# Cross attention and expert routing on one core: where VectorE picks a batch's experts

## The reference

```
scores = einsum('bhqd,bhkd->bhqk', q, k) * SCALE          # 16 heads of 16
attn = softmax(scores); out = (attn @ v) @ o_w + o_b
x = layernorm(x + out)
logits = x @ gate_w                                       # 8 experts
w, sel = top_k(softmax(logits), 2); w = w / sum(w)
routed = sum over the two chosen experts of w * swiglu_e(x)
```

## Time and profile before

| what | value |
|---|---|
| median of 3 runs | 997.99 us (994.1 to 998.68) |
| profiled execution | 1004.03 us, span of its instructions 1002.2 us |
| TensorE busy | 880.7 us, 88% |
| VectorE busy | 633.7 us, 63% |
| ScalarE busy | 433.4 us, 43% |
| GpSimd busy | 342.8 us, 34% |
| mean granted clock of TensorE | 0.95 |

### The profile page before, as it was taken

How to read it: one execution, slowest core, us unless ns; L and a number is a source line. 1 busy time by engine, 2 the same in 40 slices (tenths; PEclk the granted TensorE clock), 3 DMA queues, 4 the chain that set the end, 5 groups by cost and what they waited for, 6 DMA issues and landing times.

```text
span 1002.2 us, 18341 instructions
## 1 busy us (share of the span) xinstructions
PE 880.7 (88%) x6859; PEld 660.2 (66%) x6859; DVE 633.7 (63%) x1488; ACT 433.4 (43%) x781; POOL 342.8 (34%) x318
## 2 busy tenths in 40 slices
PE   6799788869988888899889998979997999999995
PEld 5576566657766665778656555555785777777774
DVE  5799797666898988852656778773553343333255
ACT  5688555345545444543134444445331322222221
POOL 9322201022544545630201223223631142222584
PEclk9999899777989998899889999999998999999998
DMA  5699589966443323122995112000402222221411
GB/s 167 212 302 334 168 239 331 259 158 133 102 94 70 95 60 74 57 67 78 344 380 176 51 56 85 23 23 23 153 11 91 59 64 62 61 62 55 148 66 63
DMA packets 144247, 126.71 MB, mean 126 GB/s; under 512 B 89568, under 2 KB 126112, under 8 KB 142368
## 3 DMA queue, kind: packets, MB, share of 16 engines
q1 hardware_dynamic: 140320, 113.02, 38.3%
q0 software_dynamic: 3408, 9.38, 2.5%
q10 hardware_dynamic: 432, 3.15, 0.8%
HBM read 77.23 MB, written 48.29 MB: 125 GB/s over the span
## 4 chain that ended last, share of the span: by engine, by line
PE 62%; DVE 16%; POOL 7%; ACT 7%; issue 4%; DMA 3%; SPq 0%; another core or an unknown queue 0%; POOLq 0%; DVEq 0%; ACTq 0%
PE ps L2484 9%; PE ps L1890 6%; PE ps L2499 5%; DVE cross_room L1923 3%; PE ps L1325 3%; PE ps L2348 3%; PE ps L1830 3%; PE ps L666 3%; POOL hank L345 2%; PE ps L1952 2%; PE ps L1591 2%; PE ps L423 2%; POOL kept L2631 2%; PE ps L2361 2%; DVE big L1377 2%
## 5 line engine op out<-in xcount | busy, mean ns | idle before, releaser
L1968 ACT ACTIVATE cross_room<-ps 128x1024 f32<-128x1024 f32 x64 | 65.5, 1023 | 100.3 <-PE ps L1894 98.4
L1923 DVE TENSOR_REDUCE cross_room<-ps 128x4 f32<-128x1024 f32 x64 | 78.0, 1223 | 39.6 <-PE ps L1890 38.8
L2484 PE MATMUL ps<-wr,xbT 128*128 x312 | 100.5, 465 | 1.8 <-ACT xbT L2520 1.8
L1890 PE MATMUL ps<-kept,cross_room 32*128 32x256 f32 x512 | 74.1, 411 | 21.8 <-DVE cross_room L1923 18.9
L2573 POOL DMA_INDIRECT y_dram<-yb,dest_row x39 | 37.4, 960 | 136.3 <-DVE dest_row L2549 132.1
L1293 POOL TENSOR_TENSOR st<-st,exponent 128x20 f32<-128x20 f32 x16 | 56.5, 3534 | 72.1 <-DVE st L1268 70.8
L2484 PEld LDWEIGHTS ps<-wr,xbT 128*128 128x128 f32 x312 | 59.4, 191 | 30.1 <-issue 3.5
L1894 PE MATMUL ps<-cross_room,kept 32*128 32x256 f32 x512 | 75.3, 413 | 0.0
L1890 PEld LDWEIGHTS ps<-kept,cross_room 32*128 32x128 f32 x512 | 47.2, 191 | 39.8 <-issue 19.1
L550 DVE SCALAR_TENSOR_TENSOR room<-room 128x256 f32<-128x256 f32 x144 | 58.3, 479 | 11.3 <-ACT room L499 11.3
L2558 DVE TENSOR_TENSOR cross_room<-cross_room,ps 128x352 f32<-128x352 f32 x39 | 20.3, 521 | 60.3 <-PE ps L2484 58.8
(11 more groups left out here) (349 smaller groups left out, 2264.9 us busy)
## 6 DMA issues: line engine op xcount, KB each, us to landing
xs_dram<-params SPq DMA_DIRECT2D x17, 1040.0 KB, 18.5
room<-in_gW SPq DMA_DIRECT2D x8, 1280.0 KB, 6.9
hank<-rt_dram SPq DMA_DIRECT2D x8, 1024.0 KB, 9.4
tok_dram<-room SPq DMA_DIRECT2D x8, 768.0 KB, 5.5
paths<-fir_dram SPq DMA_DIRECT2D x48, 128.0 KB, 3.8
xb<-xs_dram SPq DMA_DIRECT2D x39, 130.0 KB, 2.4
hank<-rt_dram SPq DMA_DIRECT2D x8, 552.0 KB, 10.8
yr<-y_dram SPq DMA_DIRECT2D x16, 256.0 KB, 3.6
```

The lines of the kernel that those rows point to most:

```text
L1890: m1 = nc.tensor.matmul(ps[:, c, t * T:(t + 1) * T], strips(qS[b % 3], g, c)[:, t * P:(t + 1) * P], kS(b, g)[c * CH:(c + 1) * CH], start=T ...
L1923: V.tensor_reduce(mx[:, :, g, XD + 2 * h * CH:XD + (2 * h + 1) * CH + 1:CH].rearrange("p t c -> p c t"), ps[:, pair(h), :].rearrange("p c ...
L1968: S.activation(pT[g % 2][:, pair(h)].rearrange("p c k t -> p (c k t)"), ps[:, pair(h), :].rearrange("p c n -> p (c n)"), ACT.Exp).then_inc ...
L2484: m = nc.tensor.matmul(ps[:, 2 * (j % 2) + half, 0:FF], xbT[j % 2][:, k, :], wr[:, bass.ds(e, 1), k, half, :].rearrange("p e n -> p (e n)" ...
```

## The change

The choice leaves `dve_place` and goes to the end of `dve_output`, as `dve_choose(b)`, in round 8 of the step in which the logits are made: behind the maximum of slot 7 and ahead of the maximum of slot 0 of the next step. Its instructions are the same, and none is on another engine or queue. `dve_place` keeps an empty round 0, so that weights, one-hot rows and ranks (now `dve_weigh(b)` and what follows) stay in their rounds.

```diff
@@ dve_output
                 V.tensor_scalar(y[i][:, t, 0:D], y[i][:, t, 0:D], mv[:, t, 0:1], mv[:, t, 1:2], ALU.subtract,
                                 ALU.mult).then_inc(*s.applied.up())
             yield
+            yield
+            yield
+            dve_choose(b)
+            yield
@@
-        def dve_route(b):
+        def dve_choose(b):
 
             i = b % 2
             dve.wait_ge(s.lg_turned, b + 1)
@@
             V.tensor_copy(tif[:], ti[:]).then_inc(*s.route.up())
             V.tensor_scalar(y[i][:, :, C_ID], env.row_no[:], float(b * T), None, ALU.add).then_inc(*s.route.up())
-            yield
+
+        def dve_weigh(b):
+
+            i, k = b % 2, 11 * b
             dve.wait_ge(s.ex2, b + 1)
             V.tensor_scalar(wsel[:, :, 0:1], wsel[:, :, 1:2], 1.0, None, ALU.add).then_inc(*s.route.up())
@@ dve_place
             i, k = b % 2, 7 * b
             filled = env.filled
-            yield from dve_route(b)
+            yield
+            dve_weigh(b)
```

## The result

Kernel before 998.68 us (median of 11 runs, 994.1 to 1006.08), changed kernel 1011.55 us (11 runs, 1001.99 to 1018.95): ratio 1.011, 95% interval 1.0068 to 1.0153. The forecast was 995.5 us, 2.5 us less, which is too little to be told from no change. The ratio leaves out the three of the eleven runs that lie over 1.5% above the fastest, and the profiled execution (1017.29 us, span 1015.5, 13.3 more than the span of before) is one of these three.

A forecast was written before the change was run, and what follows sets the result against it. The prediction took the cross attention's loop of scores, VectorE's maximum and next scores as the bound. Gains of 0.15 + 0 + 1.7 + 0.33 + 0.34 = 2.5 us off the median of 997.99 gave 995.5 us, range 990.5 to 1000.5.

The forecast's parts named there:

- The sum, 2.5 us: Gains at the step ends in the cross attention added up: 0.15 + 0 + 1.7 + 0.33 + 0.34, bounds 1.2 to 2.8 us.
- end of step 3: Slot 0's maximum 0.20 us late, slot 1's maximum earlier by 0.13 to 0.19 us, taken as 0.15.
- step 4: At its end slot 1's scores wait for ScalarE's exponential and VectorE already stood idle: gain 0.
- step 6: At its end slot 1's maximum can start when its scores are ready, 633.75 against 634.08: gain 0.33 us.
- step 7: At its end slot 1's maximum can start earlier, 660.65 against 660.99: gain 0.34 us.
- behind step 8: At the ends of steps 8, 9 and 10 the choice fits into VectorE's idle waits: gain 0.
- step 5: At its end L2127's 1.87 us hold by GpSimd's L1696 goes: gain 1.7 us, bounds 1.0 to 1.9.
- The choice (600.58 to 601.75) is hidden with 0.86 us to spare.: End of step 5: the choice fits between the logits' end at 600.53 and slot 0's maximum at 602.61, without delaying it.
- held among the transfers: Rival, chance 0.12: VectorE's choice is held through two of GpSimd's indirect transfers, 3.7 us slower, 1001.7 us.
- all of it comes back: Rival, chance 0.13: VectorE alone bounds the loop, four step ends give the whole choice, 6.36 us, 991.6 us.
- The rule of the Trainium skill: Shared SBUF ports: VectorE's two-input operations block only against GpSimd's SBUF reads; moved L2127 isn't blocked, L2146 and L2149 are.
- Within 0.5%: 0.77: Chance that the whole kernel's time stays between 993.0 and 1003.0 us; faster 0.17, slower 0.06.

The follow-up runs named there:

- g2: Kernel before, nothing edited, run again on the same chip as g1: 999.73 us, ratio 0.9993 to the kernel before.
- g1: Changed kernel, nothing edited, run again (4 runs) against the kernel before on the same chip: 995.72 us, ratio 0.9892.
- e6: Kernel before, nothing edited, run again in the same launch as e7: 1001.75 us, ratio 1.0002 to the kernel before.
- e7: Changed kernel, nothing edited, run again against the kernel before on the same chip: 1002.59 us, ratio 1.0014.
- e5: Kernel before with GpSimd's scatter of a batch held until slot 0's maximum of the next step is done: 992.25 us, ratio 0.9926 to the kernel before.
- f4: Changed kernel with only the logits' copy in the last round, the rest of the choice in the next step's first round: 995.65 us, 1.0011 of the kernel before.

## Why the prediction was wrong, by its own steps

- **The sum, 2.5 us.** In a launch with hand-overs in time the terms came out: end of step 3 0.20 (forecast 0.15), step 4 0.00 (0), step 6 0.37 (0.33), step 7 0.36 (0.34), behind step 8 nothing. Only step 5 was mis-sized there: 3.81 us for 1.7. The forecast's trace held L2127 for 1.87 us, g2's for 2.95; slot 1's maximum gained 2.88 us (+6.90 to +4.02), and the fall of TensorE's clock that followed in g2 did not come.
- **The step that failed: "The choice (600.58 to 601.75) is hidden with 0.86 us to spare."** It took the gap of 2.28 us as a fixed span into which 1.17 us fits. The gap was made of late hand-overs of TensorE beside the scatter (with them in time the same maximum stands at +1.22, in g2), of the logits too (choice at +0.75, not +0.24), and the maximum moved on to +3.04: 0.76 late in place of 0. No record tells what ends the gap, so why the maximum moved with the choice stays open. The text named this gap as unexplained and gave it 0.20 us at worst; it was 0.76 for VectorE and 2.15 for ScalarE (+2.34 to +4.49).
- **What wasn't in it at all:** ScalarE. Slot 1's scores wait for the exponential of slot 0 as well as for its maximum. And the clock: TensorE, idle for 3.37, 3.33 and 3.78 us at the ends of steps 5, 6 and 7, came back at 0.79 to 0.80 us a pair for 0.48. The three steps that begin there are longer by 1.96 + 3.71 + 3.29 = 8.96 us, which is the 8.8 of steps 3 to 10 and the 0.2 gained ahead of them.
- **The rival "held among the transfers", 1001.7 us, 0.12.** It had the place and the sign but not the mechanism: it wanted VectorE's operations stretched. L2131 took 0.14 and L2133 0.17 us among the transfers; VectorE was idle, not held. Its point of decision, 1.5 us at each end, was passed by ScalarE's 2.15.
- **The rival "all of it comes back", 991.6 us.** Where nothing comes late two medians (993.39 and 994.71) lie between it and the forecast and two (995.72 and 996.64) above the forecast, so the medians don't decide. Its 2.85 us for step 5 was nearer than my 1.7; at the ends of steps 3, 6 and 7 its 1.17 was too much (0.20, 0.37, 0.36).
- **The rule of the Trainium skill** (SBUF — State Buffer, section "SBUF: two separate sides") held: the two-input L2127 ended with L1696 (599.74 and 599.71 in g2), L2146 with L1699 (605.97 and 605.95 in g1), L2157 with L1703 (606.85 and 606.82), and L2131 among the transfers wasn't blocked. Of the one-hot rows that the prediction took for blocked, L2157 (L2149 before) was; L2154 (L2146 before) took 0.18 us, between two of GpSimd's pieces. The same section of the Trainium skill says that VectorE's two-port modes keep GpSimd from writing descriptors, and here that has nothing to show: behind the first of a batch the transfers took 0.96 us at a pitch of about 1.27 in every trace, with or without the choice between them.
- **The chances.** "Within 0.5%: 0.77" took the spread of one kernel's runs as the only uncertainty. Six launches of one text gave ratios of 0.989 to 1.011.

Shown: the lateness comes with a launch, in both kernels alike (e6 with e7, g1 with g2), goes where the scatter goes (e5), and is absent at the end of step 3, which has no scatter. It isn't the same at every scatter: at the end of step 4 of the result's trace the transfers run too, and maximum (+1.42) and exponential (+2.62) are in time as in every launch; only the copy L1839 comes 1.03 us late (+4.58, in g1 +3.55). Shown too that the change gains 3.8 us at one step end by getting L2127 away from L1696 (f4, g1, g2). Argued only: that the first comparison's 1% is the lateness and the clock's fall, since one execution of it was traced, the second slowest of eleven, and the other late launch (e7) came out level. Open: why one launch has late hand-overs and another not (the five chips differ, each was seen in one launch only, and the first comparison may have run on any); whether issuing or bytes make them; and why the choice, put ahead of them, makes ScalarE's exponential 0.7 to 2.15 us later still (e7 against e6 and the result against the first trace).

## What to carry to other kernels

A gap that no row explains isn't cover. Before work is put into it, find what ends it, and ask who else waits for the same thing. Where GpSimd's transfers and its elementwise work run beside a tight loop between TensorE, VectorE and ScalarE, try moving these first: holding the transfers for one maximum made either version 0.5 to 0.75% faster than the kernel before, in each of the three launches in which it was tried, and left the order of VectorE's work worth 1 us. Then look which of the two paid: in the launches in time it was GpSimd's L1696, moved away from VectorE's small operation. And if the result can go either way by launch, one comparison isn't enough: run the same text again on another chip before explaining it.

## What the runs showed of the hardware

- The end of a TensorE record and the start of its waiter can stand over 3 us apart with the waiter idle: L1894 done at 603.15, the exponential L1968 at 606.57, in the result's trace; in g1 they stand 0.21 us apart (598.78 and 598.99).
- The same program shows this in two of six launches, though its transfers are issued at the same places (-1.28, +0.11, +1.38 and +2.64 us behind the last L2015) and take the same 0.96 us behind the first.
- An operation of VectorE's of 0.14 us took 1.87, 2.95 and 3.14 us beside GpSimd's L1696 and ended with it each time (the first trace, g2, f4). In g1 L2140, with one input, took 0.47 us in place of 0.16 and ended with L1696 too (604.57 and 604.53).
- TensorE came back from a wait of 3.37 us at half clock (0.80 us a pair for 0.48), and the windows from 606 to 614 show 0.53 and 0.62. The length of one wait doesn't tell: in e7 it came back from 2.52, 2.54 and 2.94 us at 0.48 us, and in e6 from 1.83 us at 0.48 and, one slot on, from 0.21 us at 0.79.
